# A four-layer transformer on one Trainium2 core: preparing the first feed-forward group of layers 2 and 3 inside the last attention steps

## What is computed

```python
# layer 2 (c is the condition of each sequence)
x = x + g_msa * attention(modulate(layernorm(x), sh_msa, sc_msa), W_qkv, W_out, b_out)
x = x + g_mlp * (gelu(modulate(layernorm(x), sh_mlp, sc_mlp) @ W1 + b1) @ W2 + b2)

# layer 3 (q and k are rotated; 16 heads of 16)
nx = ada_rmsnorm(x, time_emb, w_norm1, ...)
x = x + attention(rotate(nx @ wq + bq), rotate(nx @ wk + bk), nx @ wv + bv) @ wo + bo
nx = ada_rmsnorm(x, time_emb, w_norm2, ...)      # x * rsqrt(mean(x*x) + eps) * g + b
x = x + (gelu(nx @ w_gate) * (nx @ w_up)) @ w_down
```

## Time and profile before

| | us |
|---|---|
| median of 3 runs | 2702.59 (2701.26 to 2704.95) |
| the profiled execution, its time | 2700.78 |
| its span, first to last instruction | 2699.0 |
| PE busy | 2493.8 (92%) |
| DVE busy | 1733.8 (64%) |
| ACT busy | 1191.5 (44%) |
| POOL busy | 495.3 (18%) |
| mean granted TensorE clock | 0.964 of full |

### The profile page before, as it was taken

One profiled execution on the slowest core, in us unless ns is written; L12 is line 12 of the kernel. 1 busy time (PEld: TensorE's weight loads), 2 busy tenths in 40 slices (PEclk: granted clock), 3 DMA queues, 4 the chain that ended last, 5 costly groups with the idle time before them and its releaser, 6 DMA issues.

```text
span 2699.0 us, 63343 instructions
## 1 busy us (share of the span) xinstructions
PE 2493.8 (92%) x25441; PEld 1939.2 (72%) x25441; DVE 1733.8 (64%) x3886; ACT 1191.5 (44%) x2456; POOL 495.3 (18%) x472
## 2 busy tenths in 40 slices
PE   6998799999999957998999999997999699879999
PEld 5876466666666546887888888886676587668888
DVE  5888787887887775554554555445554498955554
ACT  5886455655655502332333323333333477623322
POOL 1333000100100105653111110111000355500000
PEclk9999899999999957998999999998999899989999
DMA  6000000000000043344000000000000133200000
GB/s 215 3 3 2 20 23 31 23 23 28 27 23 23 21 118 112 104 133 127 25 0 0 0 0 0 0 1 1 0 1 1 44 115 112 88 8 9 16 16 16
DMA packets 72162, 102.22 MB, mean 38 GB/s; under 512 B 10881, under 2 KB 50305, under 8 KB 71489
## 3 DMA queue, kind: packets, MB, share of 16 engines
q1 hardware_dynamic: 65856, 91.46, 10.5%
q0 software_dynamic: 6144, 8.56, 1.7%
HBM read 67.20 MB, written 32.80 MB: 37 GB/s over the span
## 4 chain that ended last, share of the span: by engine, by line
PE 80%; DMA 7%; DVE 6%; issue 2%; ACT 2%; POOL 2%; SPq 1%; DVEq 0%; ACTq 0%; POOLq 0%
PE psW L322 17%; PE psW L315 9%; PE psP L1419 8%; PE psS L1556 8%; DMA rotated<-work 6%; PE psP L437 4%; PE psP L430 4%; PE psS L1548 4%; PE psO L1419 4%; PE psW L529 3%; PE psS L381 3%; PE psO L414 3%; PE psO L346 2%; PE psP L397 2%; PE psW L1419 2%
## 5 line engine op out<-in xcount | busy, mean ns | idle before, releaser
L322 PE MATMUL psW<-r,work 128*128 128x512 f32 x1024 | 481.7, 604 | 1.0 <-DVE work L782 1.0
L1284 POOL TENSOR_TENSOR work<-work 128x512 f32<-128x512 f32 x128 | 132.0, 1042 | 1132.3 <-DVE work L816 1132.3
L322 PEld LDWEIGHTS psW<-r,work 128*128 128x128 f32 x1024 | 180.7, 191 | 162.5 <-issue 156.8
L315 PE MATMUL psW<-work,r 128*128 128x128 f32 x2048 | 244.9, 279 | 1.0 <-DVE work L782 1.0
L315 PEld LDWEIGHTS psW<-work,r 128*128 128x128 f32 x2048 | 236.3, 194 | 3.5 <-DVE work L782 1.4
L1556 PE MATMUL psS<-r,work 128*128 128x256 f32 x992 | 217.3, 379 | 0.0
L1556 PEld LDWEIGHTS psS<-r,work 128*128 128x128 f32 x992 | 187.8, 190 | 25.2
L1419 PE MATMUL psP<-work,r 128*128 128x256 f32 x768 | 192.7, 388 | 13.5 <-DVE work L1625 12.8
L1198 ACT ACTIVATE work<-work 128x512 f32<-128x512 f32 x128 | 80.1, 626 | 276.4 <-DVE work L795 276.4
L1789 ACT ACTIVATE work<-psP 128x512 f32<-128x512 f32 x64 | 38.2, 597 | 325.1 <-PE psP L1419 325.1
L1419 PEld LDWEIGHTS psP<-work,r 128*128 128x128 f32 x768 | 147.9, 194 | 38.7 <-DVE work L1625 14.0
(11 more groups left out here) (308 smaller groups left out, 5060.5 us busy)
## 6 DMA issues: line engine op xcount, KB each, us to landing
r<-in_l_fc SPq DMA_DIRECT2D x16, 1024.0 KB, 6.8
rotated<-work SPq DMA_DIRECT2D x60, 256.0 KB
work<-mod_rows SPq DMA_DIRECT2D x64, 128.0 KB, 2.8
work<-rotated SPq DMA_DIRECT2D x30, 256.0 KB
r<-in_l_w SPq DMA_DIRECT2D x2, 3072.0 KB, 14.5
x<-in_x SPq DMA_DIRECT2D x8, 512.0 KB, 9.8
gather_table<-work SPq DMA_DIRECT2D x32, 128.0 KB, 1.9
moe_sum<-work SPq DMA_DIRECT2D x32, 128.0 KB, 1.7
```

What stands on the lines that cost most here:

```text
L315: ins = nc.tensor.matmul(ps[:, q * P:(q + 1) * P], w[:, k, lo + q * P:lo + (q + 1) * P], L.hT[:, k, :], start=(k == 0), stop=(k == KC - 1))
L322: ins = nc.tensor.matmul(ps[:, 0:width], L.hT[:, k, :], w[:, k, lo:lo + width], start=(k == 0), stop=(k == KC - 1))
L1284: nc.gpsimd.tensor_tensor(E, E, halves(L.rs)[i].unsqueeze(2).broadcast_to([P, 8, N]), ALU.mult).then_inc(L.s[f"prob{i}"].sem, 1)
```

## The change

- Layer 2: the roots of 28 tiles are formed in step 29, group 0 is normalised at the end of step 30 (DVE), turned in step 31 (PE) and modulated there, ahead of the last tile's `dve_l2_y`. The last tile's y goes to the bank pair psS in place of psP, and its turning back is put behind the products B0, B1 and A0 of group 0. The roots of the last four tiles are formed inside group 0.
- Layer 3: POOL forms the first four roots in step 12 (`pool_first_rms`), ACT normalises one tile in each of steps 26 to 29, PE turns group 0 in step 30, DVE modulates it in step 31, ahead of `output(31)`. The last `project` stands behind B0, A0, C0 and D0. The other 28 roots are formed inside group 0, and group 1 is normalised behind them, later than before.
- The waits `following("l2")` and `following("l3")` go from DVE and ACT, and on PE move into group 0. POOL keeps its own.
- The buffers of group 0 (xn, gT, mix) move to places that attention doesn't use.

The diff, cut to what is spoken of (functions that were only lifted out of others to be called from two places are left out, since their text is unchanged):

```diff
+        def out_bank(L, t):
+            return psS if L.li == 2 and isinstance(t, int) and t == NT - 1 else psP
...
@@ pe_attention, step
                 else:
                     finish_before()
+                    if L.li == 2:
+                        after(pe, L.s["v"], NT)
+                        for k in range(KC):
+                            pe_ff_turn(pe, Q["l2"], 0, k)
                 pe_transpose_probs(pe, L, t)
...
             def last():
-                pe_turn_out(pe, L, NT - 1)
                 if L.li == 1:
+                    pe_turn_out(pe, L, NT - 1)
                     pe_l1_logits(pe, L, NT - 1)
@@ pe_narrow
+                if rotary and t == NT - 2:
+                    after(pe, L.s["v"], NT)
+                    for k in range(KC):
+                        pe_ff_turn(pe, Q["l3"], 0, k)
             outputs(NT - 1)
             project(NT - 2)
-            project(NT - 1)
+            if not rotary:
+                project(NT - 1)
@@ new on POOL, called in step 12 of layer 3
+        def pool_first_rms(g):
+            mean, var = moments[:, 0:4, 0], moments[:, 0:4, 1]
+            nc.gpsimd.tensor_tensor(shift[:, 0:4], mean, mean, ALU.mult).then_inc(su["product"], 1)
+            nc.gpsimd.tensor_scalar(shift[:, 4:8], var, EPS, None, ALU.add).then_inc(su["biased"], 1)
...
+            nc.gpsimd.tensor_tensor(shift[:, 0:4], shift[:, 0:4], shift[:, 4:8], ALU.add).then_inc(su["product"], 1)
...
+            nc.gpsimd.tensor_tensor(rstd[:, 0:4], shift[:, 0:4], power[:, 0:1].broadcast_to([P, 4]), ALU.pow
+                                    ).then_inc(su["root"], 1)
@@ dve_narrow
+                if rotary and t == NT - 1:
+                    dve_ff_modulate(v, ch, Q["l3"], 0)
...
             output(NT - 1)
-            for t in (NT - 2, NT - 1):
-                add(t)
-                measure(t)
+            add(NT - 2)
+            if rotary:
+                dve_first_sum(v, Q["l3"], 0, 0)
+            measure(NT - 2)
+            add(NT - 1)
+            measure(NT - 1)
@@ dve_attention, step of layer 2
                 next_input()
+                if t == NT - 3:
+                    dve_rsqrt(ch, rstd[:, 0:NT - 4], moments[:, 0:NT - 4, 1])
+                if t == NT - 2:
+                    dve_ff_norm(v, ch, Q["l2"], 0, 0)
+                if t == NT - 1:
+                    dve_ff_modulate(v, ch, Q["l2"], 0)
                 dve_l2_y(v, ch, L, t)
@@ act_narrow
+                if L.li == 3 and NT - 6 <= t < NT - 2:
+                    if t == NT - 6:
+                        a.wait_ge(su["root"], 7)
+                    r = t - (NT - 6)
+                    ins = nc.scalar.activation(Q["l3"].xn[:, r, :], x[:, r, :], ACT.Copy, scale=rstd[:, r:r + 1])
+                    if r == 3:
+                        ins.then_inc(Q["l3"].s["f_xn"].sem, 1)
@@ pe_ff, hidden of layer 3
                     B(0)
                     A(0)
+                    if t == 0:
+                        after(pe, L[3].s["on"], NT)
                     C(0)
                     D_(0)
+                    if t == 0:
+                        pe_narrow_project(pe, L[3], NT - 1)
                     B(1)
                     A(1)
                     E(0)
                     D_(1)
+                    if t == 0:
+                        following(pe, "l3")
@@ pe_ff, hidden of layer 2
                 A(0)
+                if Q.kind == "l2" and t == 0:
+                    pe_turn_out(pe, L[2], NT - 1)
@@ dve_ff, hidden of layer 3
             def hidden_l3(t, ahead):
-                c11(t, 0)
-                if ahead:
-                    norm(t + 1, (t + 1) % 2)
+                if t > 0:
+                    c11(t, 0)
+                    norm_next(t, ahead)
                 c11(t, 1)
+                if t == 0:
+                    mean, var = moments[:, 4:NT, 0], moments[:, 4:NT, 1]
+                    ch.link(nc.vector.tensor_tensor(rstd[:, 4:NT], mean, mean, ALU.mult))
+                    ch.link(nc.vector.tensor_tensor(rstd[:, 4:NT], rstd[:, 4:NT], var, ALU.add))
                 c22(t, 0)
                 left_product(t, 0)
                 c22(t, 1)
+                if t == 0:
+                    dve_rsqrt(ch, rstd[:, 4:NT], rstd[:, 4:NT])
+                    norm_next(t, ahead)
                 c12(t, 0)
@@ dve_ff, end of the hidden part of layer 2
+                if Q.kind == "l2" and t == 0:
+                    dve_rsqrt(ch, rstd[:, NT - 4:NT], moments[:, NT - 4:NT, 1])
@@ dve_ff, start
-            if Q.kind != "moe":
-                dve_rstd(ch, rms=Q.kind == "l3")
-            norm(0, 0)
-            modulate(0)
+            if Q.kind == "moe":
+                norm(0, 0)
+                modulate(0)
```

More of the change, by code:

```diff
@@ L1318, in __init__ @@
                     self.w1, self.w2 = None, [l3_down] * 2
-                    spare = Region(r1)
-                    extra = [[spare.take(F) for _ in range(3)]] * 2
                 if kind == "l3":
@@ L1579, in dve_ff, with dve_first_sum @@
+        def dve_first_sum(v, Q, t, m):
+            out = Q.held[m % 2][0] if Q.kind == "l3" else Q.hidden_at(m, 0)
+            after(v, *Q.product(t, "A", m))
+            after(v, *Q.part(t, "p1", m))
+            nc.vector.tensor_tensor(out, two(BANK_C), out, ALU.add).then_inc(Q.s["f_summed"].sem, 1)
         def dve_ff(v, ch, Q):
@@ L1639, in c11 @@
             def c11(t, m):
-                out = places(t, m)[0]
-                after(v, *Q.product(t, "A", m))
-                after(v, *Q.part(t, "p1", m))
-                nc.vector.tensor_tensor(out, two(BANK_C), out, ALU.add).then_inc(Q.s["f_summed"].sem, 1)
+                dve_first_sum(v, Q, t, m)
             def c12(t, m):
```

156 lines of the change are left out of this document (88 added, 68 removed).

## The result

| | before | changed |
|---|---|---|
| median of the runs, same chip, us | 2704.95 (2701.26 to 2708.74, 5 runs) | 2687.67 (2682.27 to 2693.46, 5 runs) |
| ratio, 95% interval | | 0.9943 (0.9928 to 0.9958) |
| the profiled execution / its span | 2700.78 / 2699.0 | 2682.27 / 2680.5 |
| mean granted TensorE clock | 0.964 | 0.966 |

The change is faster by 17.3 us between the medians and by 18.5 between the profiled spans. 2683.8 was predicted for the median, in a range of 2676 to 2691, and 18.8 for the gain.

What follows compares the result with a forecast made beforehand. PE is busy 92% of the span, so time lies only where it idles or runs at half clock. Layer 2's 8.2 plus layer 3's 10.6 make 18.8 us, from 2702.59 to 2683.8; range 2676 to 2691.

Steps and rivals of the forecast that it cites:

- Layer 2's new wait: Layer 2, before group 1's turn: DVE's four normalisings held up by POOL's weight sums, PE waiting 4.4 us.
- a split of the bandwidth: Layer 2, DVE beside POOL: if they shared bandwidth, normalising would take 5.1 us again and `result` begin at 1874.6.
- The half clock behind that wait: Layer 2, from group 1's turn to `result`: TensorE at half clock after the pause, costing 2.1 us.
- Step 29's roots: Layer 2, step 29: 12 root instructions ahead of `dve_l2_y` delay PE, losing 1.0 us (bounds 0 and 1.8).
- Step 31's turn: Layer 2, step 31: eight transposes in PE's 4.50 us wait cost nothing; up to 0.6 might come back, 0 taken.
- Layer 3, ahead of the first product: Layer 3's attention end: modulation moved into step 31, first product at 2365.45 instead of 2379.72, 14.3 us earlier.
- Layer 3, group 0: Layer 3, first product to `result`: 31.8 us instead of 28.1, from `project` 0.9 and later DVE work 2.8.
- The median: Whole kernel: 18.8 us gained from 2702.59, giving a median of 2683.8.
- The first: Layer 2: POOL holds DVE up no longer than before; total gain 24.3 to 25.3, median 2678; chance 0.20.
- The third: First groups: clock stays at half throughout, 38 us more in layer 3's group 0, 2719 in all; chance 0.02.
- the second: Layer 3's attention: additions slow its loop or early turns hold up scores; gain 12, median 2691; chance 0.08.
- The fourth: Both passages: first product still waits for the whole of x, so no gain, 2702 to 2704; chance 0.02.

Runs made afterwards that it cites:

- The two experiments on the sums: Changed kernel with POOL's layer 3 weight sums started after group 1's normalising, or cut into eight half-width instructions; medians 2675.69 and 2680.18 us.
- All ten kernels with layer 2's half: The changed kernel and the follow-up kernels that keep its layer 2 part; medians from 2672.10 to 2697.11 us.
- the one without it: Changed kernel with layer 2's passage put back to what it was, layer 3's part kept; median 2692.86 us, 0.9962 to the kernel before.
- roots on POOL: Changed kernel, but POOL takes eight roots in step 12, not four, and DVE normalises group 1 at the end of layer 3's attention; 2687.93 us, 0.9935.
- the later sums: Changed kernel, but POOL starts layer 3's weight sums only when group 1 of layer 2 is normalised; 2675.69 us, 0.9892 to the kernel before.
- the 24 fillers: Changed kernel plus transposes nobody reads: 24 behind layer 2's turn of group 0, 8 and 12 more in layer 3; 2682.20 us, 0.9926 to the kernel before.

## Why the prediction was right

**Layer 2's new wait: right, in place and size.** x releases POOL, predicted for 1863.2, at 1863.60; the normalisings predicted at 8.4 took 8.21, PE's wait predicted at 4.4 was 4.33. That the normalisings go through one by one between POOL's instructions was read from two lengths of DVE. The two experiments on the sums show it: take POOL away, and they take 1.75; cut its instructions in half, and they take 5.23. The Trainium skill ("SBUF — State Buffer", section "SBUF: two separate sides") calls the port pair an exclusive lock held for the whole instruction. The 5.23 agrees with it, and speaks against a split of the bandwidth, under which the halves had changed nothing. The 8.21 alone doesn't: the prediction had 5.1 for a split, but in the row of 5.10 POOL ran beside the first two instructions only, which took 1.78 and 2.39; four at that pace would be 8.3 by a split, too.

**The half clock behind that wait: right.** 2.1 was taken, from bounds of 0 and 2.7; from the turn to `result` it took 6.92 for 4.77, that is 2.15.

**Step 29's roots: right.** 1.0 was taken, from bounds of 0 and 1.8. From the scores of tile 30 to those of tile 31 it is 17.82 before and 18.70 in the changed kernel:

```profile
1825.96 1.16 PE L381 MATMUL psS<-work 64*64 64x64 f32 x64
...
1843.78 1.16 PE L381 MATMUL psS<-work 64*64 64x64 f32 x64
```

```profile
1825.30 1.16 PE L382 MATMUL psS<-work 64*64 64x64 f32 x64
...
1844.00 1.16 PE L382 MATMUL psS<-work 64*64 64x64 f32 x64
```

All ten kernels with layer 2's half have 18.69 to 18.71, and the one without it 17.82. So 0.9 is lost for certain.

**Step 31's turn: the wrong sign of a small term.** "If the shorter idle stretch also keeps the clock up, up to 0.6 comes back; I take 0." The eight transposes shortened the pause from 4.50 to 3.63 and the clock fell all the same, at 1851.3 for 1849.7, and stayed there for 6.8 us in place of 3.4. So y took 5.38 for 3.84: 1.5 lost. Small errors the other way make up a third of that. The first product came 589.6 behind the start of the attention, for 589.4 predicted, because this execution had gained 1.0 ahead of the scores of tile 0, by an earlier rise of the clock. From those scores on the layer gained 7.2, and in the kernel with the same layer 2 and the longer half clock (roots on POOL) 6.3. So the 8.2 came out as predicted by luck: the mechanism as written gives it, but it lacks the loss at y, and the profiled execution happened to put 1.0 beside that.

**Layer 3, ahead of the first product: right.** 14.2 for 14.3, and 14.6 where the edit acts, from POOL's last masking to the first product (14.69 for 29.29). Nothing of what was added to the attention loop shows: POOL's roots were caught up in one step, ACT's four normalisings took 0.50 to 0.54 each, and the loop 234.6 for 234.9, though a loss of a microsecond or two would hide in its spread.

**Layer 3, group 0: right.** 31.7 for 31.8. The waits were 0.92 at C2 and 1.35 at E2, 2.3 for 2.8; taking away what makes them gave 2.84. "Half clock at its start as before" held in this execution by chance: it lasted 5.7 us into the group here, 5.8 before, but 3.0 with the later sums, though nothing was changed in layer 3 there.

**The median.** The gain between the medians was 17.3, 1.5 less than the stretches show. The median of 2687.67 lies 3.9 above the forecast, of which 2.4 are that the kernel before had 2704.95 in this comparison, and not 2702.59.

**The rivals.** The first (the normalisings are not held up) is what the later sums made true by another way: PE waits nothing and 7.1 us are saved, where I had 5.5 to 6.5 for it. The third did not happen, and of the second no step shows a trace, within the spread of the loop. The fourth is excluded by y and the first product in one row.

## What to carry to other kernels

When work moves, look at who is released by the same count as the moved work's successor: here the last tile of x released GpSimd into the four VectorE instructions that had become urgent, and a wait moved by one line was worth as much (7.1) as the change in its whole layer (7.2). Long GpSimd instructions beside VectorE belong where VectorE has slack, or in short pieces. A pause of TensorE that is half filled is not a filled one: look at the granted clock of what follows. And cut executions at clean edges before comparing them, since the untouched stretches here differed by up to 9.3 us from one execution to another: an edge is clean when the untouched stretch behind it has the same length in every run, as the 504.88 from tile 0's scores has, and the layer's first matmul was not one.

## What the runs showed of the hardware that I had not expected

- More work in a pause of TensorE, and a longer stretch at half clock behind it: with 4.50 us idle ahead of L397, the clock was at half for 3.4 us; with 1.04 of transposes and 3.63 idle, for 6.8 to 10.2 us in six kernels. With 2.78 of transposes more it stayed at 1.00.
- PE had 7.32 of 9 us busy from 2354 to 2363 and the clock stayed at 0.50 all the while.
- VectorE instructions of 128x4 elements are held up by GpSimd as the long ones are: 1.56 and 2.20 us, for 0.17. L682, between the two, took 0.17: it began at 1876.12, in the gap between one instruction of POOL's, ended at 1876.06, and the next, begun at 1876.13.
- The eight transposes and the 24 fillers went at 0.12 to 0.13 us each (2.78 / 24 and 1.04 / 8) at full clock, where some 5 us had been expected for the 24.
